# Gate weights of four experts spread over partitions by transfers instead of one-hot products, in a fused vision tower

## The reference, cut to what matters

```
h = h + attention(layernorm(h))
e = layernorm(h)                                     # (8, 1025, 64)
w = softmax(mean(e, axis=0) @ Wr + br)               # gate weights, one row of 8 per token place
a = relu(bn(e @ W1[k] + b1[k]))                      # layer 1, for each expert k
c = relu(bn(a @ W2[k] + b2[k]))                      # layer 2
y = c @ Wo[k] + bo[k]                                # layer 3
h = h + sum over k of y[k] * w[:, k]
```

## Time and profile before

| what | us |
|---|---|
| median of 3 runs | 371.85 (370.04 to 372.61) |
| the profiled execution, time | 371.4 |
| the profiled execution, span from first to last instruction | 369.6 |
| PE busy | 348.3 |
| DVE busy | 270.8 |
| ACT busy | 199.9 |
| POOL busy | 132.8 |

### The profile page before, as it was taken

How to read it: one execution, slowest core, us unless ns; L and a number is a source line. 1 busy time by engine, 2 the same in 40 slices (tenths; PEclk the granted TensorE clock), 3 DMA queues, 4 the chain that set the end, 5 groups by cost and what they waited for, 6 DMA issues and landing times.

```text
span 369.6 us, 7961 instructions
## 1 busy us (share of the span) xinstructions
PE 348.3 (94%) x2696; PEld 167.9 (45%) x2696; DVE 270.8 (73%) x583; ACT 199.9 (54%) x404; POOL 132.8 (36%) x201
## 2 busy tenths in 40 slices
PE   4889999999999999999999999799999999999985
PEld 2665335445545545545545655445554333333321
DVE  3221966979989989989999999968735467666662
ACT  0224547547657657657567588665675343445310
POOL 7041120644644643653652654625505600000000
PEclk9999999999999999999999999999999999999999
DMA  5999650911900900900000000000000011110012
GB/s 147 222 219 201 132 117 2 207 23 39 194 0 28 199 1 7 218 2 0 0 2 3 2 0 2 1 2 2 1 3 0 2 30 28 30 28 13 20 30 57
DMA packets 28991, 20.44 MB, mean 55 GB/s; under 512 B 12280, under 2 KB 28832, under 8 KB 28960
## 3 DMA queue, kind: packets, MB, share of 16 engines
q1 hardware_dynamic: 28352, 19.91, 26.7%
q10 hardware_dynamic: 608, 0.12, 0.2%
HBM read 17.93 MB, written 2.10 MB: 54 GB/s over the span
## 4 chain that ended last, share of the span: by engine, by line
PE 80%; DVE 4%; issue 4%; DMA 4%; ACT 3%; POOL 2%; SPq 1%; DVEq 0%; POOLq 0%; ACTq 0%
PE Sp L1417 13%; PE Sp L1564 7%; PE MM L1701 7%; PE PTB L1679 7%; PE PTB L1429 6%; PE MM L1472 6%; PE MM L1346 6%; PE MM L1349 5%; DMA XW<-in_x_dram 4%; PE MM L1480 3%; PE MM L1323 2%; PE PTB L1395 1%; PE MM L1327 1%; POOL st L481 1%; PE Sp L1721 1%
## 5 line engine op out<-in xcount | busy, mean ns | idle before, releaser
L1417 PE MATMUL Sp<-eT,G 64*64 64x512 f32 x512 | 63.9, 600 | 0.2 <-issue 0.2
L451 POOL TENSOR_SCALAR_AFFINE_SELECT EP<-EP 128x128 f32<-128x128 f32 x64 | 23.0, 360 | 103.9 <-ACT EP L656 103.9
L593 ACT ACTIVATE PT<-PTB 128x512 f32<-128x512 f32 (+3 forms) x88 | 38.7, 485 | 27.2 <-PE PTB L1429 24.6
L950 DVE TENSOR_SCALAR_CACHE_REDUCE EP<-Sp,sr 128x1024 f32<-128x1024 f32 x32 | 40.3, 1279 | 4.9 <-PE Sp L1417 4.8
L950 DVE TENSOR_SCALAR_CACHE_REDUCE SN<-Sp,sr 128x1024 f32<-128x1024 f32 x32 | 39.9, 1277 | 2.6 <-PE Sp L1417 2.6
L1417 PEld LDWEIGHTS Sp<-eT,G 64*64 64x64 f32 x512 | 18.6, 132 | 30.5 <-issue 30.3
L1244 DVE SCALAR_TENSOR_TENSOR EP<-PTB,negc,PTd 128x512 f32<-128x512 f32 x28 | 19.7, 746 | 14.0 <-PE PTB L1679 14.0
L1472 PE MATMUL MM<-PT,e 128*64 128x512 f32 (+3 forms) x168 | 29.9, 491 | 0.0
L960 DVE SCALAR_TENSOR_TENSOR SN<-SN,EP 128x384 f32<-128x384 f32 (+7 forms) x32 | 27.4, 855 | 3.4 <-POOL EP L451 2.1
L960 DVE SCALAR_TENSOR_TENSOR EP<-EP 128x128 f32<-128x128 f32 (+7 forms) x32 | 27.3, 853 | 2.1 <-ACT EP L659 1.9
L1564 PE MATMUL Sp<-E2T,W1f 64*64 64x512 f32 x224 | 28.6, 602 | 0.2 <-ACT XW L701 0.2
(11 more groups left out here) (342 smaller groups left out, 689.6 us busy)
## 6 DMA issues: line engine op xcount, KB each, us to landing
XW<-in_x_dram SPq DMA_DIRECT2D x6, 1024.0 KB, 11.0
X<-in_x_dram SPq DMA_DIRECT2D x6, 1024.0 KB, 9.7
out_dram<-xc SPq DMA_DIRECT2D x8, 256.0 KB, 2.6
XW<-in_x_dram SPq DMA_DIRECT2D x2, 576.0 KB, 8.7
X<-in_x_dram SPq DMA_DIRECT2D x2, 576.0 KB, 14.8
XW<-in_x_dram SPq DMA_DIRECT2D x2, 448.0 KB, 11.8
X<-in_x_dram SPq DMA_DIRECT2D x2, 448.0 KB, 13.2
EP<-in_L_tok_W_dram SPq DMA_DIRECT2D x2, 144.0 KB, 3.1
```

The costliest lines, as they stand in the source:

```text
L451: pool.affine_select(out=blk_, in_=blk_, compare_op=ALU.is_ge, fill=0.0, base=0, pattern=[[-1, 128]], channel_multiplier=1).then_inc(tri_d ...
L593: return act.activation(dst, src, ACT.Copy)
L950: dve.tensor_scalar(W4[p % 4], Sp[p % 2][:, :], -SCALE, sr[q][:, place(t), 0:1], ALU.mult, ALU.min, accum_out=negm[q][:, t:t + 1]).then_in ...
L1417: ins = pe.matmul(Sp[p % 2][64 * s:64 * s + 64, CH * c:CH * c + CH], G[q][rows, 128 * t + 64 * s:128 * t + 64 * s + 64], eT[q][rows, :], **ON)
```

## The change

- `weight_rows(2)` and `weight_rows(3)` and their two ACT copies are removed. `weight_rows(0)` and `weight_rows(1)` stay.
- SP waits until both copies of wT are done and then issues eight transfers from SBUF to SBUF. Each reads one partition row of wT (512 floats, 2 KB) 64 times and writes it to 64 partitions of WB, so 128 KB each. Four serve pair 2 (semaphore ld_wb[0], waited for at 64), four pair 3 (ld_wb[1]). The source rows in their order are 4, 13, 5, 12 and then 6, 15, 7, 14.
- DVE waits for these semaphores ahead of gated(0, 2) and, ahead of the class token's sum and gated(0, 3), for the second.
- ACT instead of DVE copies the bias rows to wob, between its copies for pairs 0 and 1. Those who waited for DVE's step wait for ACT's.
- On PE, layer1(12) takes the place of weight_rows(2) and layer1(13) that of weight_rows(3); they are no longer behind the class token's transpose and in the turn of b = 1, and each later unit of layer 1 stands one place earlier. On ACT, layer 1's evictions 12 and 13 move likewise.

The core of the diff (the renamed steps and waits of the tables, of POOL's wait and of PE's waits for q_wbc are left out):

```diff
--- before.py
+++ after.py
@@ -287,8 +289,8 @@
 
         NCH = 12
 
-        L1_AT = {b: (range(10 + 3 * b, 12 + 3 * b), range(12 + 3 * b, 13 + 3 * b)) for b in range(1, 5)}
-        L1_AT.update({5: (range(25, 27), range(27, 29)), 6: (range(29, 31), range(31, 32)), 7: ((), ())})
+        L1_AT = {b: (range(11 + 3 * b, 13 + 3 * b), range(13 + 3 * b, 14 + 3 * b)) for b in range(2, 7)}
+        L1_AT.update({1: (range(14, 16), range(16, 17)), 7: ((), ())})
 
         def l2_bank(b, p):
 
@@ -365,6 +367,14 @@
                 load_x(2 * j, 0)
                 load_x(2 * j + 1, 1)
 
+            sp.wait_ge(act_steps, nth("q_wTa", 1))
+            sp.wait_ge(dve_steps, nth("q_wTd", 1))
+            for i in range(NDMA, NPAIR):
+                for half in range(2):
+                    for c in range(2):
+                        row = NEXP * c + 2 * i + (1 - half if c else half)
+                        sp.dma_start(WB[64 * half:64 * half + 64, 2 * i + c, :], wT[row:row + 1, :].unsqueeze(1).to_broadcast([1, 64, CH])).then_inc(ld_wb[i - NDMA], 16)
+
             def store(b, q):
                 sp.wait_ge(o_done, at(b + 1))
                 dst = out[bass.ds(b, 1), 1:1 + S, :].rearrange("a (t p) d -> p (a t) d", p=128)
@@ -868,18 +878,23 @@
             act.wait_ge(pe_steps, nth("q_wT", 1))
             copy(wT[:, 0:256], M0[:, 0:256]).then_inc(act_steps, 1)
             copy(wTc[:, :], M0[0:NEXP, 256:384]).then_inc(act_steps, 1)
-            for i in range(NPAIR):
+            for i in range(NDMA):
                 act.wait_ge(pe_steps, nth("q_bc", i + 1))
                 copy(WB[:, 2 * i:2 * i + 2, :], Sp[i % 2][:, :].rearrange("p (e s) -> p e s", e=2)).then_inc(act_steps, 1)
+                if i == 0:
+                    act.wait_ge(pe_steps, nth("q_wb", 1))
+                    copy(wob[:, 0:NT, :].rearrange("p (c i) d -> p i c d", c=2), M0[:, :].rearrange("p (i c d) -> p i c d", c=2, d=D))
+                    copy(wob[:, NT, :], M1[:, 0:D]).then_inc(act_steps, 1)
 
             def y_copy(b):
                 act.wait_ge(l3_ready, at(4 * b + 4))
                 act.wait_ge(tr_ready, at(b - 1))
                 copy(yT[b % 2][:, :], Q0 if b == NB - 1 else M1).then_inc(y_done, 1)
 
+            h1_wide(12)
             act.wait_ge(pe_steps, nth("c_l3", 1))
             copy(yTc[:, :], M1[0:64, 128:136]).then_inc(act_steps, 1)
-            h1_wide(12)
+            h1_wide(13)
             e2t_copy(NB - 1, Sp[1])
             for b in range(1, NB):
                 y_copy(b - 1)
@@ -1256,11 +1271,11 @@
                                   yP[b // (NB - 1)][0].rearrange("p (i c d) -> p i c d", c=2, d=D),
                                   Hb(b).rearrange("p (c i) d -> p i c d", c=2), ALU.add).then_inc(o_done, 1)
 
-            dve.wait_ge(pe_steps, nth("q_wb", 1))
-            dve.tensor_copy(wob[:, 0:NT, :].rearrange("p (c i) d -> p i c d", c=2), M0[:, :].rearrange("p (i c d) -> p i c d", c=2, d=D))
-            dve.tensor_copy(wob[:, NT, :], M1[:, 0:D]).then_inc(dve_steps, 1)
             for p in range(NPAIR):
-                dve.wait_ge(act_steps, nth("q_bcc", p + 1))
+                if p < NDMA:
+                    dve.wait_ge(act_steps, nth("q_bcc", p + 1))
+                else:
+                    dve.wait_ge(ld_wb[p - NDMA], 64)
                 if p == 3:
                     dve.wait_ge(pe_steps, nth("c_tr", 1))
                     dve.wait_ge(hw_done, 1)
@@ -1554,9 +1569,9 @@
                     pe.wait_ge(pt_done, free)
                 else:
                     pe.wait_ge(h1_done, 2 * n - 2)
-                if n == 12:
-                    pe.wait_ge(act_steps, nth("q_bcc", 3))
-                if n == 13:
+                if n in (12, 13):
+                    pe.wait_ge(act_steps, nth("q_bcc", n - 11))
+                if n == 15:
                     pe.wait_ge(e2t_done, NB)
                 for s in range(2):
                     for c in range(2):
@@ -1835,9 +1850,9 @@
             pe.matmul(M1[:, 0:D], wTc[:, :], bo2[0:NEXP, 0, :], **ON).then_inc(pe_steps, 1)
             weight_rows(1)
             layer2(0, 1)
-            weight_rows(2)
+            layer1(12)
             layer2(0, 2)
-            weight_rows(3)
+            layer1(13)
             pe.wait_ge(t_done, 4)
             pe.wait_ge(pool_steps, nth("c_t", 1))
             for e in range(NEXP):
@@ -1847,12 +1862,11 @@
             layer2(0, 3)
             pe.wait_ge(act_steps, nth("c_y", 1))
             pe.transpose(M1[0:8, 192:192 + D], yTc[:, :], ident[0:64, 0:64]).then_inc(pe_steps, 1)
-            layer1(12)
             layer3(0, 0)
             layer3(0, 1)
 
             def last_turn():
-                pe.wait_ge(act_steps, nth("q_bcc", 4))
+                pe.wait_ge(h1_done, 28)
                 pe.wait_ge(e2_done, NB)
                 for i in range(QG):
                     ins = pe.transpose(L1p[1][0][:, 128 * i:128 * i + 128], e32[0][:, 2 * i:2 * i + 2, :], ident[:, :])
```

More of the change, by code:

```diff
@@ L236, in tower @@
         st_out = [sem(f"st_out{i}") for i in range(2)]
+        NDMA = 2
+        ld_wb = [sem(f"ld_wb{i}") for i in range(NDMA, NPAIR)]
         once = {
@@ L244, in tower @@
                 bn_row bn_neg bn_neg bn_neg bn_neg bn_c2 bn_c2 c_ag c_ag c_vecc c_vecc
-                k_exp k_sq t_uac t_ubc t_sqA q_cmc q_cmc q_x7c t_sqB q_x7c q_exp q_wTa q_wTc q_bcc q_bcc q_bcc q_bcc c_y""".split(),
+                k_exp k_sq t_uac t_ubc t_sqA q_cmc q_cmc q_x7c t_sqB q_x7c q_exp q_wTa q_wTc q_bcc q_wbc q_bcc c_y""".split(),
             "dve_steps": """c_sum c_mean c_cent wef_done wef_done wef_done c_ss c_e0 c_w00p c_w00
@@ L248, in tower @@
                 t_hA t_hA t_hA t_hA t_meanA t_centA k_e2 t_hB t_hB t_hB t_hB t_ssA t_meanB t_centB
-                t_ssB c_hs c_ha c_h1 q_lga q_x q_add q_mx q_sub t_e c_m c_m q_sum q_rc q_w q_w q_wc q_wTd q_wbc""".split(),
+                t_ssB c_hs c_ha c_h1 q_lga q_x q_add q_mx q_sub t_e c_m c_m q_sum q_rc q_w q_w q_wc q_wTd""".split(),
             "pe_steps": """a_ready bn_T c_e0T bn_rows c_vec q_bo k_r0T t_ua t_ub t_oa t_ob k_eT q_x7 c_l1 q_x7 q_lc q_lg c_l2
-                q_wT q_bc q_wb q_bc q_bc q_bc c_l3 c_tr""".split(),
+                q_wT q_bc q_wb q_bc c_l3 c_tr""".split(),
         }
@@ L581, in _ @@
             pool.tensor_tensor(t2c[:, :, :], t2c[:, :, :], bc(gw9[0:64, NT, :], 8), ALU.mult).then_inc(pool_steps, 1)
-            pool.wait_ge(dve_steps, nth("q_wbc", 1))
+            pool.wait_ge(act_steps, nth("q_wbc", 1))
             pool.tensor_tensor(h2c[:, :], h2c[:, :], wob[0:8, NT, :], ALU.add).then_inc(hw_done, 1)
@@ L1666, in layer2 @@
                 elif b == 0 and p == 1:
-                    pe.wait_ge(dve_steps, nth("q_wbc", 1))
+                    pe.wait_ge(act_steps, nth("q_wbc", 1))
                 elif b == 0 and p == 2:
```

## The result

| | before | changed |
|---|---|---|
| median, first comparison (4 and 4 runs) | 371.33 us | 389.83 us (386.25 to 392.36) |
| ratio | | 1.0467, interval 1.042 to 1.0515 |
| median, second comparison on one chip (13 and 4 runs) | 370.73 us | 385.28 us (385.13 to 387.87) |
| ratio | | 1.0422, interval 1.0384 to 1.0459 |

The change makes the kernel slower by 4.2 to 4.7%. The forecast was 382.4 with a range of 369.5 to 402. The ratio of the first comparison leaves out one slow run of the changed kernel, the profiled one (392.36 us); its median takes in all four.

What follows compares the result with a forecast made beforehand. PE was taken to bound the kernel while DVE hands it tiles in time. Span 359.75 + 20 (moving) + 0.5 (clock) = 380.2, plus 1.8 = 382.0 profiled; median, 0.45 above, 382.4 us; range 369.5 to 402.

Steps and rivals of the forecast that it cites:

- What bounds, and what PE saves: PE bounds turn and loop; two weight_rows groups leave its chain, 2.12 us; span 367.85 if transfers are in time.
- Bias rows at zero: ACT copying the bias rows instead of DVE, before its pair 1 copy, costs nothing: zero, +-0.1 us.
- The formula, 359.75 + M: Span once DVE's wait for pair 3 ahead of the class token's sum holds PE, M being moving time; floor 367.85.
- M: Time to move the eight transfers' 1.05 MB into WB; taken as 20 us, range 4.8 to 38.3.
- The first of its two readings: One source row gives 27 GB/s, a geometric mean; two neighbours read side by side give 55 GB/s, 19.1 us.
- the two bounds: Transfer rates: at best 219 GB/s (4.8 us of moving), at worst 3.4 GB/s for one source row (306 us).
- The second reading: From the cls_tok broadcast, 128 reads in 5.2 us: the transfers' 512 reads take 20.8 us at the same cost.
- The clock: Some PE groups after the wait run at a lower granted clock: between 0 and 3 us, 0.5 taken.
- Rival 1: Transfers run like loads of x, landing by 284.0; span 367.85, median 370.1; chance 0.22 with landings about in time.
- Rival 2: Transfers served one behind the other, each at 27 GB/s: 38.3 us, median 401; chance 0.22 with what lies between.

Runs made afterwards that it cites:

- e1: Changed kernel, but each of the eight transfers reads 64 different partitions of wT instead of one 64 times: 370.12 us, ratio 0.9986.
- e4: Kernel before, with only ACT instead of DVE copying the bias rows, no transfers: 371.27 against 371.19 us, ratio 1.0012.
- r1_after_again: The changed kernel once more, unaltered, on the same chip as the runs beside it: 385.28 us.
- e2: Changed kernel, but all eight transfers read partition row 4: 401.99 us, ratio 1.0845.
- e6: Changed kernel, but wT's 16 rows are first written to HBM and the eight transfers read them there: 371.34 us, ratio 1.0009.
- e5: Changed kernel plus seven unread products on PE ahead of layer2(0, 3) and seven ahead of layer3(0, 0): 384.81 us beside 385.28.
- e3: Changed kernel, but every second transfer reads the copy of its row 64 partitions higher in wT: 384.22 us, ratio 1.0357.
- e8: Changed kernel, but only pair 3 by transfers (four), weight_rows(2) back, layer1(12) and layer1(13) moved, class token's sum ahead of the wait: 374.02 us, ratio 1.0085.

## Why the prediction was right, and where its sizes were off

The direction, the place and the order of size were right; the measured rise was 14.6 us in the second comparison and 18.5 in the first, against 10.6.

**What bounds, and what PE saves.** Right. With the waits gone (e1) the span was 367.8 against 367.85 worked out. Two errors of 0.5 us cancel in it. First, layer3(0, 0) starts at 287.15 and not 287.65, since the groups of layers 1 and 2 in a row start 0.86 us apart there (at 282.10, 282.96 and 283.82) and not 1.02 to 1.06.

Second, from layer3(0, 0) to the end it takes 80.65 and not 80.2. Half of this is PE's start after a gap, the uncovered sum of the class token: its first sixteen products take 1.95 in place of 1.72. The other half is that the group of layer 1 which left this part was worth less than the 1.02 I gave it. It was one of two in a row, which together took 1.88 us at 338.87 in the chain before, where e1 has one of 1.02 at 337.86, and the group of layer 2 behind it grew from 0.86 to 0.98: 0.74 us in all. **Bias rows at zero**: nothing in e4 speaks against it.

**The formula, 359.75 + M.** It carried. In r1_after_again the copies of wT ended at 277.1, 0.5 earlier than in the profile before. With M = 21.7 measured in place of 20, 82.4 - 80.2 = 2.2 in place of 0.5 for what follows the wait (1.7 of it the clock, 0.5 as in e1), and 0.5 less at the start, the predicted span of 380.2 becomes 383.1; it was 383.0.

**M.** 20 taken, 21.7 measured (8% off). The first of its two readings was sound: 27 GB/s for one source is what e2 measures (moving 38.6 us, 38.3 worked out), and two neighbours in the queue are nearly read side by side (56 GB/s in the middle of r1_after_again). That the geometric mean of the two bounds hit it is luck; the number came from no mechanism. It gave 19.1 us for two rows side by side all the time, and that is what failed in it: r1_after_again has 29 GB/s in the first 4 us and 22 in the last 2, with 56 between. For the same reason pair 2 did not land half way but 13.6 us after the first issue, and PE's two waits were 7.2 and 6.1 us long and not some 4 and 8; their sum, 13.3, is close to the 12 foretold. The second reading, 128 reads of a broadcast row in 5.2 us, gave the right number for a wrong reason: e6 reads rows of HBM 64 times over at 195 GB/s. What it was that held cls_tok's load up remains open; the loads of x beside it and its small pieces of 256 bytes are two candidates that no run separates.

**The clock.** The term was mis-sized: 0.5 taken, 1.7 (e5 against r1) to 2.6 us measured, inside the bounds of 0 to 3. My reason, that the share below full was small in the earlier trace rows, read the end of the kernel as if it were a mean; the stretch was cut off by the end of the span. After PE's two waits the clock was at half for 3.5 us (r1_after_again) to 5 us (the first profile) of full work.

**Rival 1** (source for nothing) fell; that about 219 GB/s stood in the rows was true of loads and stores over 64 and 128 partitions. With 64 source rows the transfers within SBUF moved 200 GB/s (e1), and with one row 27 (e2). No run shows a limit of a port or of the engines as such, the two that the rival sets against each other. **Rival 2** (one after the other) holds for one source row, with 38.6 us of moving (e2) for its 38.3, and not for rows 4 to 7 and 12 to 15 in turn, with 21.7 (r1_after_again). There the rate in the middle, 56 GB/s against the 27 of one row, shows that a transfer was in part read beside the one ahead of it.

**What lies between 385.3 and 389.8** is open. The profiled execution of the first comparison, 392.4 us, lost time ahead of the transfers. There the granted clock is 0.50 to 0.97 in stretches at 16 to 20, 32 to 44 and 276 to 284 us, and the copies of wT end 6.4 us later than in the second profile. PE was busy throughout the stretches from 277 to 281 us, and the clock was at 0.54 to 0.50 in those from 278, so a wait right ahead isn't the only thing after which the clock is found low. The other three executions have no trace. The kernel before has executions with a lower mean clock too (374.5 and 375.5 us, both at 0.984, among its 13). Whether the change makes them more frequent is open.

## To carry to other kernels

Spreading a row over partitions by a DMA out of SBUF was bound here by the place where the row lies. With the same bytes, pieces and destinations the eight transfers moved 27 GB/s from one row (e2), 48 from rows 4 to 7 and 12 to 15 in turn (r1_after_again) and 200 from 64 rows (e1). Before products are replaced by a transfer, work out from which time on the transfer costs (here 8.1 us for a saving of 1.8), and take the wait's effect on PE's clock as a term of its own (here 1.7 to 2.6 us). Where a step is moved, look what had been hidden beneath the old order: here the class token's sum came out from beneath layer1(12), and in e1 PE stood idle for 0.36 us before layer3(0, 0), out of the 2.1 saved.

## What the runs showed of the hardware that I had not expected

- SP's issues became long. A store's took 0.37 us and those of e1 0.6, but those of e2 took up to 4.78 us each, which is about the time in which 128 KB move at 27 GB/s, and each landed some 17.9 us after its issue, or nearly four such times. So it looks, by this quotient (17.9 / 4.78), as if the queue takes about four of these transfers and SP then waits for room; that is an estimate, and no run varied it. It cost nothing, as SP had nothing else to do; I had counted 3.0 us for eight issues where they took 16.7 (r1_after_again).

```profile
L376 SPq DMA_DIRECT2D PTd<-EP x8: 527/4768/4781, 276.2 to 298.8; - x8
...
DMA to landing us min/median/max: 7.2/17.9/18.3
```

- Source rows from four places in turn (e3) moved only 54 GB/s, from two 48 (r1_after_again).
- After PE had stopped at about 286.0 in e3, the clock was at 0.95 in the stretch from 287 and 0.50 from 288 us, while in e8, where PE had stopped at 290.5, it was at 0.80 in the stretch from 292 and at 0.50 from 293 us.
